# State space on VectorE: one 1024-column instruction for both channel halves of a state, and the skip term as a diagonal matmul

## The reference, cut to what matters

```python
xs = silu(conv(xs) + conv_b)                 # 4 taps along the positions
Bm, Cm = split(xs @ xp_w, 2)                 # 16 columns each
dt = softplus(Bm @ dt_w + dt_b)
A = -exp(A_log)
def step(hst, inp):                          # along the positions
    xt, dtt, Bt, Ct = inp
    dA = exp(dtt[..., None] * A)
    hst = hst * dA + dtt[..., None] * Bt[:, None, :] * xt[..., None]
    yt = sum(hst * Ct[:, None, :], -1)
    return hst, yt
y = (y + D_skip * xs) * silu(gate)
return y @ out_w + res
```

## Time and profile before

| | us |
|---|---|
| runs, median of 3 | 4943.44 (4936.61 to 4944.58) |
| profiled execution, span from first to last instruction | 4944.1 |
| VectorE busy over the program | 3465.1 (70%) |
| TensorE matmuls busy | 3835.4 (78%) |
| GpSimd busy | 2386.9 (48%) |
| ScalarE busy | 2341.8 (47%) |

### The profile page before, as it was taken

The page is one execution under the profiler, slowest core; times in us unless marked ns, Lnnn a source line. Parts: engine busy times, 40 slices in busy tenths (PEclk is TensorE's granted clock), DMA queues, the critical chain, the costliest instruction groups (busy, mean ns, idle before and its releaser), DMA issues. The chain is left out here.

```text
span 4944.1 us, 90876 instructions
## 1 busy us (share of the span) xinstructions
PE 3835.4 (78%) x25840; PEld 2735.3 (55%) x25840; DVE 3465.1 (70%) x9524; ACT 2341.8 (47%) x5537; POOL 2386.9 (48%) x3900
## 2 busy tenths in 40 slices
PE   7889797779999799568869937567775887799365
PEld 5666565656666466456646626422332665466265
DVE  7887775666666676566658856669998664588566
ACT  3444464355666466234436624345553454366243
POOL 5666442534344442446643354367776662233453
PEclk9999898789999899679979959779998999899698
DMA  6000332100000232133323311212121330133113
GB/s 234 0 0 1 112 124 76 52 20 1 0 0 1 72 124 94 39 124 107 107 80 117 110 38 47 73 48 65 63 62 64 114 117 28 51 120 112 36 46 87
DMA packets 244547, 341.24 MB, mean 69 GB/s; under 512 B 26976, under 2 KB 187120, under 8 KB 243120
## 3 DMA queue, kind: packets, MB, share of 16 engines
q1 hardware_dynamic: 230960, 309.19, 18.8%
q0 software_dynamic: 13184, 27.22, 1.6%
HBM read 182.77 MB, written 147.26 MB: 67 GB/s over the span
## 5 line engine op out<-in xcount | busy, mean ns | idle before, releaser
L522 DVE TENSOR_REDUCE l0att_rowmax<-l0att_S 128x2 f32<-128x512 f32 x512 | 339.8, 687 | 125.2 <-PE l0att_S L701 122.9
L893 POOL TENSOR_TENSOR wb_prob<-wb_prob,wb_rden 128x128 f32<-128x128 f32 (+1 forms) x512 | 248.2, 506 | 360.7 <-DVE wb_rden L1070 360.3
L522 DVE TENSOR_REDUCE l1ffn_rowmax<-l1ffn_S 128x2 f32<-128x512 f32 x512 | 337.6, 686 | 87.2 <-PE l1ffn_S L701 83.1
L1983 POOL TENSOR_TENSOR ssm_hc<-core_AW_all,ssm_Cs 128x512 f32<-128x512 f32 x256 | 320.8, 1268 | 131.2 <-DVE core_AW_all L2129 98.1
L1434 POOL DMA_INDIRECT results<-e_y,e_back x220 | 213.7, 971 | 289.4 <-DVE e_y L1662 269.9
L935 ACT ACTIVATE wb_prob<-wb_biased,wb_nmax 128x128 f32<-128x128 f32 (+1 forms) x512 | 228.6, 447 | 236.0 <-DVE wb_nmax L1063 233.6
L2228 PE MATMUL ssm_Y<-ssm_hc,core_ident 128*128 128x512 f32 x512 | 287.8, 672 | 56.8 <-POOL ssm_hc L1983 31.1
L2129 DVE TENSOR_TENSOR_SCAN core_AW_all<-core_AW_all,ssm_U 128x512 f32<-128x512 f32 x256 | 310.6, 1213 | 1.0 <-ACT core_AW_all L2072 0.6
L701 PE MATMUL l1ffn_S<-l1ffn_K,l1ffn_Q 128*128 128x512 f32 x512 | 251.0, 494 | 75.1 <-DVE l1ffn_rowmax L522 42.3
L1775 PE MATMUL e_H<-e_xT,e_W1s 128*128 128x128 f32 x1760 | 252.0, 288 | 70.2 <-issue 50.6
L701 PE MATMUL l0att_S<-l0att_K,l0att_Q 128*128 128x512 f32 x512 | 248.6, 489 | 60.4 <-DMA l0att_K<-bounce 47.5
(11 more groups left out here) (498 smaller groups left out, 11511.3 us busy)
## 6 DMA issues: line engine op xcount, KB each, us to landing
bounce<-l0att_parts SPq DMA_DIRECT2D x128, 256.0 KB, 2.8
bounce<-l1ffn_parts SPq DMA_DIRECT2D x128, 256.0 KB, 2.8
ssm_Cs<-c_rows SPq DMA_DIRECT2D x128, 256.0 KB, 3.1
routed<-core_Y SPq DMA_DIRECT2D x8, 2048.0 KB, 24.8
l0att_Q<-bounce SPq DMA_DIRECT2D x128, 128.0 KB
l0att_K<-bounce SPq DMA_DIRECT2D x128, 128.0 KB
bounce<-l1att_parts SPq DMA_DIRECT2D x64, 256.0 KB, 2.8
l1ffn_Q<-bounce SPq DMA_DIRECT2D x128, 128.0 KB
```

The costliest lines, as they stand in the source:

```text
L522: dve.tensor_reduce(out=rowmax[:, jp, qt, 2 * pair:2 * pair + 2], in_=S[a % 2][:].rearrange("p (j k) -> p j k", j=2)[:, :, 0:keys(qt)], op ...
L893: ins = pool.tensor_tensor(out=prob[:, w_ % NP, a:b], in0=prob[:, w_ % NP, a:b], in1=rden[:, w_ % NP, n:n + 1].to_broadcast([P, b - a]), o ...
L1983: pool.tensor_tensor(out=hc[:, u % 4], in0=hs[:, u % 4], in1=Cs[:, n % 4], op=ALU.mult)\
```

## The change

Inflow, scan and the product with C take both halves of a state in one instruction of 1024 columns. `BU` grows to two banks per buffer; the spread row of B goes into the second bank of the buffer that the inflow then fills, and the inflow reads it there for both halves, the second half in place. `BB` goes. `dA`, `hs` and `hc` keep their sizes, as two buffers of a state instead of four of a unit. The inflow runs just ahead of its own scan, and the spread one state ahead instead of two; it waits for the scan two states back. The skip term becomes a matmul of xs with a diagonal matrix `skip_w` (the identity scaled by D, made once on ScalarE), which opens the accumulation in `YS`; VectorE's two skip instructions in `gate` go. One wait of `split_b`, for a product of GpSimd itself, goes too.

```diff
-        BB = [ps("B0"), ps("B1")]
-        BU = [ps("U0"), ps("U1")]
+        BU = [ps("U0", (P, CT * T2)), ps("U1", (P, CT * T2))]
...
-        dA = core.AW_all[:, 0:4 * T2].rearrange("p (b t) -> p b t", b=4)
-        hs = core.AW_all[:, 4 * T2:8 * T2].rearrange("p (b t) -> p b t", b=4)
+        dA = core.AW_all[:, 0:4 * T2].rearrange("p (b c t) -> p b c t", b=2, c=CT)
+        hs = core.AW_all[:, 4 * T2:8 * T2].rearrange("p (b c t) -> p b c t", b=2, c=CT)
         Cs = sb("Cs", [P, 4, T2])
-        hc = sb("hc", [P, 4, T2])
+        hc = sb("hc", [P, 2, CT, T2])
+        skip_w = sb("skip_w", [P, CT, P])
...
@@ sync
-                        await_(sp, hc_made, CT * (g - 3))
+                        await_(sp, hc_made, g - 3)
...
@@ gpsimd
-            def weigh(r, w_):
-                n, u = r * N + w_ // CT, r * WS + w_
-                pool.wait_ge(scanned.sem, u + 1)
-                if w_ % CT == 0:
-                    pool.wait_ge(c_sent[n % 4].sem, 16 * (n // 4 + 1))
-                await_(pool, summed, u - 3)
-                pool.tensor_tensor(out=hc[:, u % 4], in0=hs[:, u % 4], in1=Cs[:, n % 4], op=ALU.mult)\
+            def weigh(g):
+                pool.wait_ge(scanned.sem, g + 1)
+                pool.wait_ge(c_sent[g % 4].sem, 16 * (g // 4 + 1))
+                await_(pool, summed, CT * (g - 1))
+                pool.tensor_tensor(out=hc[:, g % 2], in0=hs[:, g % 2],
+                                   in1=Cs[:, g % 4, None, :].to_broadcast([P, CT, T2]), op=ALU.mult)\
                     .then_inc(hc_made.sem, 1)
...
-                    if inside(r):
-                        weigh(r, w_)
+                    if inside(r) and w_ % CT == 0:
+                        weigh(r * N + w_ // CT)
...
@@ scalar
+            for c in range(CT):
+                act.activation(skip_w[:, c, :], core.ident[:], ACT.Copy, scale=core.d_skip[:, c:c + 1])\
+                    .then_inc(skip_made.sem, 1)
...
-                await_(act, scanned, u - 3)
-                act.activation(both(dA[:, u % 4])[:, :, 1:L], both(dt[:, r % 2, c])[:, :, 1:L], ACT.Exp,
+                await_(act, scanned, r * N + n - 1)
+                act.activation(both(dA[:, n % 2, c])[:, :, 1:L], both(dt[:, r % 2, c])[:, :, 1:L], ACT.Exp,
                                scale=A[:, c, n:n + 1]).then_inc(dA_made.sem, 1)
...
@@ vector
-            def inflow(u):
-                r, n, c = u // WS, u // CT, u % CT
-                if u % WS == 0:
+            def inflow(g):
+                r = g // N
+                if g % N == 0:
                     dve.wait_ge(du_made.sem, du_made.at(r, CT))
-                if c == 0:
-                    dve.wait_ge(b_made.sem, n + 1)
-                await_(dve, scanned, u - 1)
-                dve.tensor_tensor(out=BU[u % 2][:], in0=du[:, r % 2, c], in1=BB[n % 2][:], op=ALU.mult)\
+                dve.wait_ge(b_made.sem, g + 1)
+                dve.tensor_tensor(out=BU[g % 2][:].rearrange("p (c t) -> p c t", c=CT), in0=du[:, r % 2],
+                                  in1=BU[g % 2][:, None, T2:2 * T2].to_broadcast([P, CT, T2]), op=ALU.mult)\
                     .then_inc(bu_made.sem, 1)
...
-            def scan(u):
-                dve.wait_ge(bu_made.sem, u + 1)
-                dve.wait_ge(dA_made.sem, u + 1)
-                await_(dve, hc_made, u - 3)
-                dve.tensor_tensor_scan(hs[:, u % 4], dA[:, u % 4], BU[u % 2][:], 0.0, ALU.mult, ALU.add)\
-                    .then_inc(scanned.sem, 1)
+            def scan(g):
+                dve.wait_ge(dA_made.sem, CT * (g + 1))
+                await_(dve, hc_made, g - 1)
+                dve.wait_ge(bu_made.sem, g + 1)
+                dve.tensor_tensor_scan(hs[:, g % 2].rearrange("p c t -> p (c t)"),
+                                       dA[:, g % 2].rearrange("p c t -> p (c t)"), BU[g % 2][:], 0.0, ALU.mult,
+                                       ALU.add).then_inc(scanned.sem, 1)
...
-                for c in range(CT):
-                    dve.scalar_tensor_tensor(out=YS[c][:], in0=xc[:, j % 2, c], scalar=core.d_skip[:, c:c + 1],
-                                             in1=YS[c][:], op0=ALU.mult, op1=ALU.add).then_inc(skipped.sem, 1)
...
-                        u = r * WS + w_
-                        if u == 0:
-                            inflow(0)
-                        if u + 1 < TURNS * WS:
-                            inflow(u + 1)
-                        scan(u)
+                        if w_ % CT == 0:
+                            inflow(r * N + w_ // CT)
+                            scan(r * N + w_ // CT)
...
@@ tensor
-                await_(pe, bu_made, CT * (n - 1))
-                pe.matmul(BB[n % 2][:], sel[:, n % N, :], bc3[:, n // N % 2, :], start=True, stop=True)\
+                await_(pe, scanned, n - 1)
+                pe.matmul(BU[n % 2][:, T2:2 * T2], sel[:, n % N, :], bc3[:, n // N % 2, :], start=True, stop=True)\
                     .then_inc(b_made.sem, 1)
...
-                pe.wait_ge(hc_made.sem, u + 1)
+                if c == 0:
+                    pe.wait_ge(hc_made.sem, u // CT + 1)
                 if n == 0:
+                    if r == 0:
+                        pe.wait_ge(skip_made.sem, CT)
                     await_(pe, gated, gated.at(r - 1, CT))
-                pe.matmul(YS[c][:], core.ident[:], hc[:, u % 4], start=n == 0, stop=n == N - 1)\
+                    pe.matmul(YS[c][:], skip_w[:, c, :], xc[:, r % 2, c], start=True, stop=False)
+                pe.matmul(YS[c][:], core.ident[:], hc[:, u // CT % 2, c], start=False, stop=n == N - 1)\
                     .then_inc(summed.sem, 1)
...
-                    n = r * N + w_ // CT + 2
+                    n = r * N + w_ // CT + 1
```

More of the change, by code:

```diff
@@ L1876, in state_space @@
         dt_exp, log_made, dt_made, du_made = sig("dt_exp"), sig("log_made"), sig("dt_made"), sig("du_made", CT)
-        b_made, bu_made, dA_made = sig("b_made", N), sig("bu_made", WS), sig("dA_made", WS)
-        scanned, hc_made, summed = sig("scanned", WS), sig("hc_made", WS), sig("summed", WS)
-        skipped, gated, added = sig("skipped", CT), sig("gated", CT), sig("added")
+        b_made, bu_made, dA_made = sig("b_made", N), sig("bu_made", N), sig("dA_made", WS)
+        scanned, hc_made, summed = sig("scanned", N), sig("hc_made", N), sig("summed", WS)
+        skip_made = sig("skip_made")
+        gated, added = sig("gated", CT), sig("added")
         dve_step, pool_step = sig("dve_step"), sig("pool_step")
@@ L1954, in split_b @@
                 await_(pool, b_made, b_made.at(j - 2, N))
-                await_(pool, hc_made, (j - 1) * WS + max(w for w in POOL_AT if POOL_AT[w] == "split") + 1 if j else 0)
                 step(pool.tensor_copy(bc3[0:32, j % 2], bc[:]))
@@ L1971, in times_x @@
                 pool.wait_ge(activated.sem, activated.at(j, CT))
-                await_(pool, bu_made, bu_made.at(j - 2, WS))
+                await_(pool, bu_made, bu_made.at(j - 2, N))
                 for c in range(CT):
@@ L2140, in gate @@
                 for c in range(CT):
-                    dve.wait_ge(skipped.sem, skipped.at(j, c + 1))
                     dve.tensor_tensor(out=yg[:, c], in0=sg[:, j % 2, c], in1=YS[c][:], op=ALU.mult)\
@@ L2163, in _ @@
                     if r == -1 and w_ == 5:
-                        dve.memset(dA.rearrange("p b (s q) -> p (b s) q", s=2)[:, :, 0:1], 0.0)\
+                        dve.memset(dA.rearrange("p b c (s q) -> p (b c s) q", s=2)[:, :, 0:1], 0.0)\
                             .then_inc(zeroed.sem, 1)
```

## The result

| | before | changed |
|---|---|---|
| runs, median (lowest to highest), us | 4943.23 (4936.61 to 4944.58) | 4974.14 (4969.20 to 4977.89) |
| profiled span, us | 4944.1 | 4967.5 |
| state-space stage in it, us | 587.19 | 615.20 |

A forecast was written before the change was run, and what follows sets the result against it. VectorE was taken as the bound, with no hole from state to state. Six intervals +13.6, the seventh +4.1, outside them -4.7, +0.6 and +1.1 summed to +14.7 us: 4959 us, range 4935 to 4976.

The forecast's parts named there:

- seventh interval: Interval into the last turn, without statistics and `apply`: saves 4.3 us before, only 2.5 after the change, so +4.1 us.
- Width: VectorE's wide inflow 1.23 and scan 2.28 us, scan 0.03 behind inflow: period 3.46 us, a gain of 0.31 a state.
- Step 1: Inflow of state 7: its spread stands in TensorE's queue behind the convolutions; stall 4.6 us against 0.62 before.
- Step 2: Inflows of states 8 and 9: spreads behind g0, g1 and the bc matmuls are some 0.2 us late each.
- Step 3: Scan of state 12: waits for GpSimd's product of 10, behind the splitting of B; stall 1.5 us.
- Step 4: Inflow of state 13: TensorE idles 5.1 us, runs the sum of 10 at 1.2 GHz; stall 1.9 us.
- Step 5: Statistics at the next turn's start: 1.29 us, then `ssm_ve`, ending with the running GpSimd instruction, now longer.
- Step 6: Inflow of state 3 behind the gate: TensorE's skip and sum at 1.2 GHz make its spread late; stall 1.0 us.
- A: Spread of state 7 is in time: 4931 us, or 4893 with no stall at all; chance 0.12.
- B: TensorE keeps 2.4 GHz at the sum of state 10: turn 68.7 us, +3.7, so 4948 us; chance 0.18.
- C: One more clock drop, at the sum of 14, delays the product of 0 and `ssm_ve` by 1.2: 4967 us; chance 0.18.
- Rival D: Wide VectorE instructions save nothing, being exactly twice as long (1.39 and 2.43 us): 4984 us; chance 0.05.

The follow-up runs named there:

- the fillers: Changed kernel with four more zero-weight matmuls a turn on TensorE between the sums of states 9 and 10: 4965.9 us, 1.0038 times before.
- the lead given back: Changed kernel with the spread of B in its own two banks, two states ahead, and one pair of inflow banks: 4955.9 us, 1.0022 times before.
- all repairs: Changed kernel with spread of 7 between convolutions, splitting of B in three, gate one state earlier, `apply` moved, third decay buffer: 4941.4 us, 0.9993 times before.
- early gate: Changed kernel with the gate one state earlier in VectorE's order, right behind the next turn's scan of state 0: 4971.0 us, 1.0065 times before.

## Why the prediction was right, and where it was mis-sized

The sign was right, the time lies within the range but close to its upper end (forecast 4959, range 4935 to 4976, measured 4974), and the main step is in its place: the inflow waits for the spread behind the convolutions. The stage was forecast to grow by 14.7 us and grew by 28.0. An interval runs from the end of the scan of state 4 in one turn to that in the next. These are the scans of state 4 (before: of its second half) of turns 0, 6 and 7, before and after; each ends its length behind its start:

```profile
3274.17 1.21 DVE L2129 TENSOR_TENSOR_SCAN core_AW_all<-core_AW_all,ssm_U 128x512 f32<-128x512 f32 x1
...
3681.72 1.21 DVE L2129 TENSOR_TENSOR_SCAN core_AW_all<-core_AW_all,ssm_U 128x512 f32<-128x512 f32 x1
...
3746.53 1.22 DVE L2129 TENSOR_TENSOR_SCAN core_AW_all<-core_AW_all,ssm_U 128x512 f32<-128x512 f32 x1
```

```profile
3269.37 2.29 DVE L2130 TENSOR_TENSOR_SCAN core_AW_all<-core_AW_all,ssm_U 128x1024 f32<-128x1024 f32 x1
...
3702.80 2.29 DVE L2130 TENSOR_TENSOR_SCAN core_AW_all<-core_AW_all,ssm_U 128x1024 f32<-128x1024 f32 x1
...
3771.75 2.29 DVE L2130 TENSOR_TENSOR_SCAN core_AW_all<-core_AW_all,ssm_U 128x1024 f32<-128x1024 f32 x1
```

| term | forecast us | measured us |
|---|---|---|
| six intervals | +13.6 (6 x 70.3 against 6 x 68.03) | +25.9 (433.43 against 407.55) |
| of these: the first | 70.3 long | 74.5 long |
| the other five | 70.3 long each | 71.7 to 72.0 long |
| seventh interval | +4.1 | +4.1 (68.95 against 64.82) |
| outside the intervals | -3.0 | -2.0 |

- *Seventh interval*: right by luck. I had let it be 4.3 us shorter than an ordinary one before the change and 2.5 after; it was 3.1 shorter (67.93 in the mean against 64.82; among others, the skip at its gate waits 0.74 us there for TensorE's sum) and 2.8 (71.8 against 68.95). What I overrated there makes up for the growth of an ordinary turn that I underrated.
- *Width*, the first term that was mis-sized. The instructions are as priced (1.216 and 2.287 us against 1.23 and 2.28), the gap was not: a scan begins 0.13 us behind the end of its inflow, not 0.03. The period is 3.54, not 3.46; 16 x 0.085 = 1.4 us a turn. I had taken the gap from the inflow of a second half behind the scan of before, and written that an error there counts little since stalls absorb it. They absorbed part at most: those of 7, 12 and 13 are shorter by 0.8 us in sum. In the kernel before, the inflow of a second half waits for one semaphore, the scan's, and begins 0.03 to 0.04 us behind it, as the first row below does behind the scan shown in the earlier trace rows. The inflow of a first half waits for the spread as well and begins 0.10 to 0.11 behind: the scan of the second row ends at 3776.02, and the next inflow in the earlier trace rows begins at 3776.12.

```profile
3774.20 0.69 DVE L2122 TENSOR_TENSOR ssm_U<-ssm_du,ssm_B 128x512 f32<-128x512 f32 x1
3774.81 1.21 DVE L2129 TENSOR_TENSOR_SCAN core_AW_all<-core_AW_all,ssm_U 128x512 f32<-128x512 f32 x1
```

In the changed kernel the first two scans of the stage wait for two semaphores (decay and inflow) and begin 0.10 to 0.11 behind their inflow, the later ones wait for three (the product as well) and begin 0.13 behind it:

```profile
3254.37 1.22 DVE L2122 TENSOR_TENSOR ssm_U<-ssm_du,ssm_U 128x1024 f32<-128x1024 f32 x1
3255.69 2.29 DVE L2130 TENSOR_TENSOR_SCAN core_AW_all<-core_AW_all,ssm_U 128x1024 f32<-128x1024 f32 x1
...
3385.83 1.21 DVE L2122 TENSOR_TENSOR ssm_U<-ssm_du,ssm_U 128x1024 f32<-128x1024 f32 x1
3387.17 2.29 DVE L2130 TENSOR_TENSOR_SCAN core_AW_all<-core_AW_all,ssm_U 128x1024 f32<-128x1024 f32 x1
3389.38 1.21 DVE L2122 TENSOR_TENSOR ssm_U<-ssm_du,ssm_U 128x1024 f32<-128x1024 f32 x1
```

- *Step 1*: 4.50 us against 4.6, by the cause named (the queue; shown by moving the spread). *Step 2*: 0.23 at state 9, nothing at 8, against 0.2 at each. *Step 3*: 1.2 against 1.5, by the splitting (shown by cutting it in three). *Step 4*: 1.4 to 1.6 in ordinary turns against 1.9, by the half clock (shown by the fillers).
- *Step 5*: `ssm_ve` ends with GpSimd's product, as read from the earlier trace rows: 1.24 to 1.32 us in ordinary turns.
- *Step 6*, the second term that was mis-sized: 2.0 us against 1.0. I let the clock come back after 3.4 us of matmuls, the length of the one burst in the earlier trace rows. In the rows of the gate above it stayed at half for some 5.2 us of skip and sum, and the spread of 3 began 6.1 us behind their start instead of 5.1.
- The five ordinary intervals then follow: 70.3 + 1.4 + 1.0 - 0.8 = 71.9. The first, 74.5, has an inflow of 7 that waits 5.57 us, inflows of 13 and 3 that wait 0.5 and 0.4 longer than in the others, and an `ssm_ve` of 2.10 us; I had not set it apart.
- *Rivals.* A (spread in time) fell. B (clock stays up) fell; what I had written for it, that idle stretches of about 2 us end without a drop, holds for part of the rows of before only: the sum at 3453.12 there, behind 1.97 us of nothing, takes 3.30 us. C's drop at the sum of 14 occurs in six of seven turns, in five of them late in the sum (about 2.5 us). In the first turn the whole sum runs at half clock, the product of 0 waits 1.50 us for it, and `ssm_ve`, beside that product, takes 0.8 us more than in ordinary turns: C's chain is there, once. The time came out near C's 4967 by the other terms.

```profile
3320.57 3.57 PE L2227 MATMUL ssm_Y<-ssm_hc,core_ident 128*128 128x512 f32 x4 [1.64 <-POOL ssm_hc L1981]
...
3324.59 2.10 DVE L2109 TENSOR_SCALAR ssm_ve<-ssm_mv 128x4 f32<-128x4 f32 x1
```

- *Rival D* (no shorter instructions) fell as written, but 3.75 us a state with the lead given back shows it nearer than I thought: inflow and scan of a state are 0.31 us shorter in sum than the two narrow pairs, and the dependence took that back. By the Trainium skill's rule quoted with rival A (VectorE: DVE Perf Modes, The TRN2 errata) a wide inflow takes, as an estimate, (1024 + 151) / 0.96 = 1224 ns; the trace agrees, with 1216.

## What to carry to other kernels

Before two instructions are joined into one wide one, count what the buffers for the joined form take from: here a state of lead in PSUM. The waits for the spread grew by 55.6 us, and scans and inflows got 40.1 us shorter. Price the gap behind a dependence apart from the instruction, and try parts of a change alone: here the part that looked small was the one worth having. After a repair look at lengths as well as at waits, since an instruction that another engine holds shows no wait at all.

## What was not expected of the hardware

- A VectorE inflow that does not wait for the scan ahead starts 0.08 us before that one's end in the profile. An inflow or a scan that does wait for the instruction ahead starts behind its end, and the gap goes with the number of semaphores waited for, in the kernel before, the changed one and the one with the lead given back: 0.03 us for one, 0.10 to 0.11 for two, 0.13 for three. No run changed that number alone, so it is not shown to be the cause. Per state, waiting and not waiting differ by 3.75 - 3.54 = 0.21 us.
- `ssm_ve` on 4 columns took 0.17 us where no product ran on GpSimd ahead of it (with all repairs, one turn) and up to 2.3 us where one did; one of the four instructions of `apply` took 2.39 us instead of 0.33 (early gate).
- The same idle stretch of TensorE ended both ways: after 2.55 us the sum of 14 took 1.98 us, a turn later, after 2.56 us, 2.50, the clock falling to 0.50 behind it. Why was not settled.

```profile
3393.95 1.98 PE L2227 MATMUL ssm_Y<-ssm_hc,core_ident 128*128 128x512 f32 x4 [2.55 <-POOL ssm_hc L1981]
...
3465.83 2.50 PE L2227 MATMUL ssm_Y<-ssm_hc,core_ident 128*128 128x512 f32 x4 [2.56 <-POOL ssm_hc L1981]
```
